# Two expert stages of a fused kernel: own PSUM banks, weights split earlier, an unrolled loop, and column operands in a threshold search

## What is computed

```python
# layer 0: top-2 routing with capacity, 8 experts, 1024 hidden, cap = 640 rows
for e in range(8):
    match = topk_experts == e
    elig = match.any(-1) & ~fallback
    pos = jnp.cumsum(elig) - 1
    kept = elig & (pos < cap); overflow = elig & (pos >= cap)
    idx = ...                       # the tokens that hold slots 0..cap-1
    y_e = gelu(x_flat[idx] @ W1[e] + b1[e]) @ W2[e] + b2[e]
    y_flat = y_flat.at[idx].add(y_e * w[:, None])

# layer 1: expert choice, 8 experts in 4 groups, 682 hidden, 256 tokens for each expert
Sm = softmax(xf @ Wr + br)
G_t, idx_t = jax.lax.top_k(Sm.T, 256)   # each expert takes its 256 best tokens
mid = silu(einsum('keh,ehf->kef', xf[idx], W_up[group]) + b_up[group])
out = einsum('kef,efh->keh', mid, W_down) + b_down
y = zeros.at[idx].add(G[..., None] * out)
```

## Time and profile before

| | |
|---|---|
| median of 3 runs | 868.36 us (865.08 to 871.39) |
| the profiled execution | 871.3 us, of which the span of the trace is 869.6 |
| TensorE busy in the span | 642.2 us, 74% |
| VectorE, ACT, POOL busy | 59%, 48%, 39% |
| mean granted TensorE clock | 0.862 of full speed |

### The profile page before, as it was taken

The page is one execution under the profiler, slowest core; times in us unless marked ns, Lnnn a source line. Parts: engine busy times, 40 slices in busy tenths (PEclk is TensorE's granted clock), DMA queues, the critical chain, the costliest instruction groups (busy, mean ns, idle before and its releaser), DMA issues. The chain is left out here.

```text
span 869.6 us, 14738 instructions
## 1 busy us (share of the span) xinstructions
PE 642.2 (74%) x4856; PEld 475.2 (55%) x4856; DVE 515.6 (59%) x1634; ACT 415.2 (48%) x810; POOL 341.6 (39%) x474
## 2 busy tenths in 40 slices
PE   3988898378999999999424868887778630169895
PEld 3777786247768767877312445554445420047663
DVE  1477656655766575565115577777874438866653
ACT  1355422154775686576111557655656320055672
POOL 2233334364356336552312445344444230123654
PEclk9999999679999999999855789888889755579998
DMA  5253224254455355432311223222200122024543
GB/s 188 75 183 99 74 73 139 75 167 99 122 127 123 86 127 110 136 77 26 55 42 33 62 69 87 72 79 64 73 28 27 50 87 70 8 63 135 147 102 37
DMA packets 73872, 75.94 MB, mean 87 GB/s; under 512 B 8037, under 2 KB 66449, under 8 KB 73553
## 3 DMA queue, kind: packets, MB, share of 16 engines
q1 hardware_dynamic: 61217, 59.32, 21.9%
q0 software_dynamic: 10928, 15.57, 10.3%
q10 hardware_dynamic: 1664, 0.27, 0.2%
HBM read 52.20 MB, written 22.94 MB: 86 GB/s over the span
## 5 line engine op out<-in xcount | busy, mean ns | idle before, releaser
L1866 DVE CUSTOM_DVE_ANT_0 c_sn<-c_ps_s,k_mask 128x128 f32<-128x128 f32 (+1 forms) x256 | 75.8, 352 | 56.1 <-PE c_ps_s L2004 56.1
L1390 PE MATMUL b_ps_y<-b_w2h,b_hh 128*128 128x256 f16 x320 | 87.3, 273 | 6.4 <-DVE b_xl L1283 4.4
L1390 PE MATMUL b_ps_y<-b_w2h,b_hl 128*128 128x256 f16 x320 | 87.2, 273 | 0.0
L1390 PE MATMUL b_ps_y<-b_w2l,b_hh 128*128 128x256 f16 x320 | 87.2, 273 | 0.0
L1698 POOL TENSOR_SCALAR_AFFINE_SELECT c_pr<-c_pr 128x512 f32<-128x512 f32 x64 | 43.2, 675 | 108.6 <-ACT c_pr L1757 107.6
L1200 POOL DMA_INDIRECT res<-b_y,b_s_idx x40 | 69.1, 1727 | 41.7 <-ACT b_y L1242 33.0
L1274 DVE TENSOR_TENSOR b_hl<-b_h,b_hh 128x640 f16<-128x640 f32 x64 | 52.9, 826 | 38.4 <-ACT b_hh L1222 37.7
L1186 POOL DMA_INDIRECT e_xg<-rows,e_g_idx x35 | 37.0, 1056 | 90.9 <-DVE e_g_idx L1301 80.4
L2032 PE MATMUL c_ps_v<-c_pr,k_vx 128*64 128x256 f32 (+1 forms) x512 | 62.4, 369 | 5.6 <-POOL c_pr L1698 5.0
L1355 PE MATMUL b_ps_h<-b_xh,e_w1h 128*128 128x320 f16 x256 | 56.9, 304 | 4.1 <-ACT b_h L1217 3.0
L1757 ACT ACTIVATE c_pr<-c_ps_t 128x768 f32<-128x768 f32 x64 | 51.7, 807 | 13.1 <-PE c_ps_t L2018 13.1
(11 more groups left out here) (409 smaller groups left out, 1776.2 us busy)
## 6 DMA issues: line engine op xcount, KB each, us to landing
e_w<-in_L_ffn_W_dram SPq DMA_DIRECT2D x16, 1024.0 KB, 5.4
d_w<-in_L_ffn_W_down_dram SPq DMA_DIRECT2D x8, 640.0 KB
k_ks<-kT SPq DMA_DIRECT2D x48, 64.0 KB, 3.2
c_qs<-q SPq DMA_DIRECT2D x48, 64.0 KB, 2.3
d_w<-in_L_ffn_W_up_dram SPq DMA_DIRECT2D x4, 682.0 KB, 5.9
rows<-a_rows SPq DMA_DIRECT2D x8, 264.0 KB, 2.6
rows<-c_rows SPq DMA_DIRECT2D x8, 264.0 KB, 2.2
a_x_in<-in_x_dram SPq DMA_DIRECT2D x8, 256.0 KB, 3.3
```

The source lines that it names most:

```text
L1390: last = pe.matmul(ps_y[(j + CT) % 2][:, 0:D], a, b[:, f, :], start=(f == 0 and k == 0), stop=(f == FC - 1 and k == 2))
L1866: dve.tensor_tensor_reduce(sn[r][:, a:b], ps_s[:, r, a:b], mask[:, a:b], -1.0, 3.0e38, ALU.add, ALU.min, mx[g % 2][:, q, r, j:j + 1]).then ...
```

## The change

Capacity experts:

- the turned rows have banks of their own, `ps_x` and `ps_i` in turn, each holding one tile; the index matmuls share `ps_i`, wait for the last xl, and stand behind down tile j=0; VectorE's work on the indices stands behind yb(0);
- W2's split parts are double, and W2 of expert e+1 is split in the down phase of e, a piece behind each of y(0) to y(3); W1's four pieces all stand ahead of yb(0); W2 of expert 0 is split at the end of `attention_causal`; SP loads W1 and W2 an expert further ahead;
- the loop is unrolled.

Expert choice:

- three raw buffers are shared by up and down weights, in one list `WEIGHTS`; there are 3 up and 6 down pairs of split parts; the first seven weights are split while the tokens are selected: ACT scales the raw weight in place and copies it to f16, POOL subtracts; the other five are split in the loop by ACT and VectorE;
- POOL clears only the last 256 columns of each raw buffer; the load of `bd` goes behind the fourth weight and has a semaphore of its own;
- in the threshold search `cand` is made from `more`, `thr` and the next try in one operation with column operands, and `thr` is updated behind it.

```diff
 # attention_causal, end of ACT and of VectorE
+            act.wait_ge(s_w2, 16)
+            for high in down:
+                act.activation(high[1], high[0], ACT.Copy, scale=WS0).then_inc(s_wh2, 1)
...
+            for k, low in enumerate(down):
+                dve.wait_ge(s_wh2, k + 1)
+                dve.scalar_tensor_tensor(out=low[2], in0=low[0], scalar=WS0, in1=low[1], op0=ALU.mult,
+                                         op1=ALU.subtract).then_inc(s_wl2, 1)
 # experts_capacity
-        ps_x = [ps_y[k][:, 0:C * P].rearrange("p (c t) -> p c t", c=C) for k in range(2)]
-        ps_i = pb("ps_i", [P, 512])
+        ps_xi = [pb("ps_x", [P, 2, C, P]), pb("ps_i", [P, 2, C, P])]
+        ps_x = [bank[:, 1, :, :] for bank in ps_xi]
+        IDX = ps_xi[1][:, 0, 0, 0:CT]
...
-                with eng.Fori(0, E // 2 - 1) as i:
-                    step(i * 2, 0, True, True, True)
-                    step(i * 2 + 1, 1, True, True, True)
-                step(E - 2, 0, False, True, True)
-                step(E - 1, 1, False, False, True)
+                for e in range(E):
+                    step(e, e % 2, e + 2 < E, e + 1 < E, True)
 # SP
-                if products and rows:
-                    sp.wait_ge(s_wl2, (e + 1) * WP)
-                    load_down(e + 1)
-                if rows and not (isinstance(e, int) and e + 2 >= E):
+                if rows and e + 2 < E:
                     sp.wait_ge(s_wl1, (e + 2) * WP)
                     load_up(e + 2)
+                    sp.wait_ge(s_wl2, (e + 2) * WP)
+                    load_down(e + 2)
 # ACT, hidden phase, then down phase
-                        if f < WP:
-                            if f == 0:
-                                act.wait_ge(s_w2, (e + 1) * 16)
-                            act.activation(down[f][1], down[f][0], ACT.Copy, scale=WS).then_inc(s_wh2, 1)
...
+                if rows and products:
+                    act.wait_ge(s_w1, (e + 2) * 16)
+                    act.wait_ge(s_ph, (e + 1) * FC)
+                    for part in up:
+                        act.activation(part[1], part[0], ACT.Copy, scale=WS).then_inc(s_wh1, 1)
                 for j in range(CT):
...
+                    if rows and products and j < WP:
+                        if j == 0:
+                            act.wait_ge(s_w2, (e + 2) * 16)
+                        act.activation(down[v][j][1], down[v][j][0], ACT.Copy, scale=WS).then_inc(s_wh2, 1)
 # VectorE, down phase: four w1l pieces, then yb(0), then the indices, then w2l pieces
+                    if slots and j == 0:
+                        dve.wait_ge(s_pidx, e + 3)
+                        dve.tensor_copy(of(who, e + 2), IDX).then_inc(s_who, 1)
...
+                    if rows and products and j < WP:
+                        dve.wait_ge(s_wh2, (e + 1) * WP + j + 1)
+                        dve.scalar_tensor_tensor(out=down[v][j][2], in0=down[v][j][0], scalar=WS, in1=down[v][j][1],
+                                                 op0=ALU.mult, op1=ALU.subtract).then_inc(s_wl2, 1)
 # TensorE
+                def found():
+                    pe.wait_ge(s_vhi, e + 3)
+                    pe.wait_ge(s_atlo, e + 3)
+                    pe.wait_ge(s_xl, (e + 2) * CT)
...
                         if j >= 2:
                             pe.wait_ge(s_yb, e * CT + j - 1)
-                        elif rows:
-                            pe.wait_ge(s_xl, (e + 2) * CT + j - 1)
                         if j == 0:
+                            count(pe, s_yb, e * CT)
                             pe.wait_ge(s_wl2, (e + 1) * WP)
...
+                        if slots and j == 0:
+                            found()
 # experts_choice
+    RAW, UPS, DOWNS, EARLY = 3, 3, 6, 7
+    WEIGHTS = [("up", 0), ("down", 0), ("down", 1), ("up", 1), ("down", 2), ("down", 3),
+               ("up", 2), ("down", 4), ("down", 5), ("up", 3), ("down", 6), ("down", 7)]
...
+            for i in range(len(WEIGHTS)):
+                if i >= RAW:
+                    split_done(sp, i - RAW)
+                load(i)
+                if i == RAW:
+                    sp.dma_start(bd[:], ins["L1_ffn_b_down"].partition_broadcast(P)).then_inc(s_bd, 16)
...
-            for u in range(2):
-                pool.memset(w2[u][:], 0.0).then_inc(s_fill, 1)
+            for u in range(RAW):
+                pool.memset(raw[u][:, FULL * D:FC * D], 0.0).then_inc(s_fill, 1)
...
+            for i in range(EARLY):
+                full, high, low = split_of(i)
+                pool.wait_ge(s_wh, i + 1)
+                pool.tensor_tensor(low, full, high, ALU.subtract).then_inc(s_wlp, 1)
...
+                if i < EARLY:
+                    act.activation(full, full, ACT.Copy, scale=WS).then_inc(s_wsc, 1)
+                    act.wait_ge(s_wsc, i + 1)
+                    act.activation(high, full, ACT.Copy).then_inc(s_wh, 1)
+                else:
+                    act.activation(high, full, ACT.Copy, scale=WS).then_inc(s_wh, 1)
...
-                    dve.tensor_tensor(cand[:], thr[:], tries[:, n:n + 1], ALU.bitwise_or).then_inc(s_cand, 1)
...
+                    given = tries[:, n + 1:n + 2]
+                    if n:
+                        dve.tensor_scalar(cand[:], more[:], thr[:], given, ALU.bitwise_or, ALU.bitwise_or)\
+                            .then_inc(s_cand, 1)
...
-                    dve.tensor_tensor(thr[:], thr[:], more[:], ALU.bitwise_or).then_inc(s_thr, 1)
+                if n:
+                    dve.tensor_scalar(thr[:], more[:], thr[:], None, ALU.bitwise_or).then_inc(s_thr, 1)
...
-                if e >= 0:
-                    down_low(e)
...
-                if e >= 0 and e % 2 == 0 and group(e + 2) < G:
-                    up_low(group(e + 2))
+                if 0 <= e < len(WEIGHTS) - EARLY:
+                    weights_low(EARLY + e)
...
-            pe.wait_ge(s_ldb, 48)
+            pe.wait_ge(s_ldb, 32)
```

More of the change, by code:

```diff
@@ L99, in capacity_tables @@
              "w1h": sb("w1h", [P, C, F], F16), "w1l": sb("w1l", [P, C, F], F16),
+             "w2h": [sb(f"w2h{u}", [P, FC, D], F16) for u in range(2)],
+             "w2l": [sb(f"w2l{u}", [P, FC, D], F16) for u in range(2)],
              "at_lo": [sb(f"at_lo{u}", [P, NT, P], F16) for u in range(2)],
@@ L231, in attention_causal @@
                                "w2", "w1h", "w1l", "at_lo", "at_hi", "vhi", "g_idx", "xg"))
-        up = pieces(w1, w1h, w1l)
+        up, down = pieces(w1, w1h, w1l), pieces(w2, tiles["w2h"][0], tiles["w2l"][0])
         ps_x, ps_c, ps_q, ps_k, ps_v, ps_w, ps_s, ps_p = (
@@ L1096, in run @@
                 step(-1, 1, False, True, False)
-                with eng.Fori(0, E // 2 - 1) as i:
-                    step(i * 2, 0, True, True, True)
-                    step(i * 2 + 1, 1, True, True, True)
-                step(E - 2, 0, False, True, True)
-                step(E - 1, 1, False, False, True)
+                for e in range(E):
+                    step(e, e % 2, e + 2 < E, e + 1 < E, True)
             return run
         def count(eng, what, value):
-            if not isinstance(value, int) or value > 0:
+            if value > 0:
                 eng.wait_ge(what, value)
         WP = WP0
-        up, down = pieces(w1, w1h, w1l), pieces(w2, w2h, w2l)
-        assert WP <= CT and WP <= FC
+        up, down = pieces(w1, w1h, w1l), [pieces(w2, w2h[u], w2l[u]) for u in range(2)]
+        assert WP <= CT and CT % 2 == 1 and E % 2 == 0
         block = ctx.enter_context(nc.Block(no_gpsimd_drain=True))
@@ L1310, in step @@
                                              op0=ALU.add, op1=ALU.add).then_inc(s_si, 1)
+                if rows and products:
+                    for k, part in enumerate(up):
+                        dve.wait_ge(s_wh1, (e + 1) * WP + k + 1)
+                        dve.scalar_tensor_tensor(out=part[2], in0=part[0], scalar=WS, in1=part[1], op0=ALU.mult,
+                                                 op1=ALU.subtract).then_inc(s_wl1, 1)
                 for j in range(CT):
-                    if rows and products and j < WP:
-                        dve.wait_ge(s_wh1, (e + 1) * WP + j + 1)
-                        dve.scalar_tensor_tensor(out=up[j][2], in0=up[j][0], scalar=WS, in1=up[j][1], op0=ALU.mult,
-                                                 op1=ALU.subtract).then_inc(s_wl1, 1)
                     if products:
@@ L2229, in rows_of, with raw_count, split_of, split_done @@
             return P if f < FULL else LAST
+        def raw_count(i):
+            return sum(16 if WEIGHTS[k][0] == "up" else 32 for k in range(i % RAW, i + 1, RAW))
+        def split_of(i):
+            kind, n = WEIGHTS[i]
+            if kind == "up":
+                return raw[i % RAW][:, 0:C * F], wide(w1h[n % UPS]), wide(w1l[n % UPS])
+            return raw[i % RAW][:], wide(w2h[n % DOWNS]), wide(w2l[n % DOWNS])
+        def split_done(eng, i):
+            if i < EARLY:
+                eng.wait_ge(s_wlp, i + 1)
+            else:
```

(11 more changed lines are left out.)

186 lines of the change are left out of this document (79 added, 107 removed).

## The result

The changed kernel takes 843.37 us (median of 4, 842.57 to 844.16) against 868.01 for before: a ratio of 0.9715, 95% interval 0.9678 to 0.9752. It is 24.6 us faster; 847 was forecast, with 838 to 860 as the range.

What follows compares the result with a forecast made beforehand. TensorE was taken to bound the capacity loop (169.4 us busy of 179). Terms summed to -20.7 us, from the median 868.36 to 847.7, stated as 847; own range 838 to 856, 838 to 860 with (c), (b) and most of mild (a).

Steps and rivals of the forecast that it cites:

- Attention's end: End of the attention ahead of the capacity experts: gains the first expert's four down pieces, +0.5 us, bounds 0 and +2.5.
- Experts 1 to 6: Capacity loop: TensorE waits of 9.5 us removed, 2 back as a new wait on yb(0); net -7.5 us.
- Expert 0: Capacity stage, first expert: waits on b_xl (1.3) and b_yb (1.7, put to the loop's first pass) go; -3.0 us.
- Ahead of the threshold: Choice stage: shorter memsets bring the copy of scores earlier, biases' transpose waits less; -2.5 us, bounds -1.5 and -2.7.
- Threshold: Choice stage, eight-level search: the OR making cand leaves the chain, 0.1 to 0.19 us for each of seven; -1.0 us.
- POOL splits in the selection: Choice stage: for up to 5 us POOL runs beside two-input operations behind the search; +2 us, bounds 0 and +5.
- Choice loop: Choice stage: TensorE waits on d_w2l (4.5) and d_h (4.4) go, 1 us unseen; -8.5 us, bounds -4 and -11.
- Rival (a): Capacity loop: POOL's gathers and scatters become the limit; mild 848 to 866 us, chance 0.10; a loss, 877, 0.04.
- (b): Choice stage, threshold search: POOL holds up one-column operations, some 13 us lost, 2 saved behind; 858 us, chance 0.09.
- (c): Choice loop: half of the 8.9 us comes back as waits on d_xg; 852 us, chance 0.10.

Runs made afterwards that it cites:

- choice half alone: Kernel before with only the expert choice stage changed, capacity stage as before: 854.0 us, ratio 0.9848.
- loop written out alone: Kernel before with the capacity loop over pairs of experts written out and nothing else changed: 867.2 us, ratio 0.9993.
- long fills: Changed kernel with the 1536-column clears of two raw buffers and the early load of the down biases, as before: 843.2 us, ratio 0.9717.
- capacity half alone: Changed kernel's capacity part with the expert choice stage of before: 857.8 us, ratio 0.9888 to before.
- added wait: Changed kernel where TensorE's hidden phase of expert 5 in the choice stage waits for an added transfer: 849.2 us, ratio 0.9803 to before.
- old threshold: Changed kernel with the threshold search of before, cand and thr made by two-input operations from SBUF: 853.0 us, ratio 0.9802 to before.

## Why the prediction was right, and where it was off

The direction, the range and the places were right; 20.7 were summed, 24.6 came. The nearness of the sum is partly luck: by the medians of the halves the capacity stage gave less than its 10.7 (8.9) and the choice stage more than its 10.0 (12.7), though both forecasts lie within the intervals. Term by term, forecast and then what the profiles or the controlled runs have:

- **Attention's end**, +0.5: +0.1. The splits run beside the gather. The +4.6 of the whole attention is no part of the change: it varies by 8 us among kernels with the same code there, with stretches of half clock at different places.
- **Experts 1 to 6**, -7.5: -10.2 against the profile of before, -8.7 against the choice half alone. The removed waits were right, 4.6 and 3.8 by the earlier trace rows, and the table load went with the loop. The 2 us booked for a new wait on yb(0) did not come, but only just. VectorE had yb(0) ready (0.42 from 263.62) just as TensorE wanted the bank, and down j=2 started at 264.09:

```profile
...
261.21 2.49 DVE L1305 SCALAR_TENSOR_TENSOR e_w1l<-e_w,e_w1h 128x512 f16<-128x512 f32 x4
263.62 0.42 DVE L1312 SCALAR_TENSOR_TENSOR b_yb<-b_ps_y,e_b 128x256 f32<-128x256 f32 x1
...
```

```profile
...
264.09 0.28 PE L1398 MATMUL b_ps_y<-e_w2h,b_hh 128*128 128x256 f16 x1
...
```

  TensorE came later than I had it (near 5.8 to 6) and VectorE sooner (6.4): down j=0, found and j=1 took until 6.16 us into the phase and yb(0) came at 6.1, the same in each of these experts. TensorE is idle 0.09 us ahead of that matmul in experts 1 to 5, and 0.6 us in expert 6, which has no found; the 0.6 is all that the view counts. So there is no slack left here.
- **Expert 0**, -3.0: -5.0 against the profile of before, -3.1 against the choice half alone. The step that failed is its reason. The 1.7 us of the earlier trace rows was put to the loop's first pass; the choice half alone has the loop and not that wait, and its expert 0 took 33.9 us. The Trainium skill's rule on fetching behind a taken branch (page "Runtime: NRT & Kernel Launch", section "Instruction fetch mechanics"), cited for it, is borne out by no run here. What gave the 3.1 instead: 1.4 by the loop written out alone (33.9 to 32.5), by the table load, which I had given no price, and 1.7 by the place of W2 (32.5 to 30.8). Why yb(0) was late in that one execution was not looked for.
- **Ahead of the threshold**, -2.5: -2.6. The term is right where it stands; by the long fills only 0.7 of it reaches the end of the stage.
- **Threshold**, -1.0: -0.6. The new `cand` takes 0.27 us, the old one 0.159, so less of the chain went than the 0.19 of a step. VectorE's timeline has it, an `ok` and the first operation behind the search:

```profile
...
708.79 0.27 DVE L2457 TENSOR_SCALAR d_cand<-d_more,d_thr,d_tries 128x1 int32<-128x1 int32 x1
708.98 0.20 DVE L2462 TENSOR_SCALAR d_thr<-d_more,d_thr 128x1 int32<-128x1 int32 x1
...
711.49 0.16 DVE L2444 TENSOR_SCALAR d_ok<-d_cnt 128x1 f16<-128x1 f32 x1
...
729.01 1.19 DVE L2466 COPY d_thr_row<-d_thr 128x128 f32<-128x128 f32 x1
```

- **POOL splits in the selection**, +2: +0.9. POOL was done at 730.1, 1.1 us behind the search, not 5; its subtractions took 2.78 and 3.08 us, 2.0 ns a column where the earlier trace rows had 2.26:

```profile
...
709.24 6.16 POOL L2320 TENSOR_TENSOR d_w2l<-d_raw,d_w2h 128x1536 f16<-128x1536 f32 x2
...
727.35 2.77 POOL L2320 TENSOR_TENSOR d_w1l<-d_raw,d_w1h 128x1364 f16<-128x1364 f32 x1
```

  Its last one held the copy of 128x128 behind the search: 1.19 us, against 0.227 in before.
- **Choice loop**, -9.5 on TensorE and 1 back in the tail: -15.1 and 2.0 back between the two profiles. The waits went as named, 4.5 and 4.4 of the earlier trace rows; those on d_xg and d_xl stayed, 3.2 and 3.1. The term that was mis-sized is the clock. I gave it 0.6 us, for which I named no row, and between these profiles it was 5.8: the busy time of the same 700 matmuls, 82.0 to 76.2. Before had three stretches of 3.4 us at half clock inside the loop, at 782.6, 826.9 and 857.7, each behind waits; this is the first:

```profile
...
782.60:786.00 3.40, 3.28 (x30) 2.66 (x31) 2.50 (x4) 1.97 (x2) 0.00 (x0) 0.50 0.67 205
...
```

  But this is the price of that execution and not of the waits. The loop written out alone has the choice stage of before, and its profile has the same waits (5.3 and 4.8 us in place of 4.5 and 4.4), 15.1 us of idle time in all in place of 14.0, and half clock only in the first 4.4 us of the choice loop. Its whole loop, then the 3.4 us behind its longest wait:

```profile
...
763.54:855.95 92.41, 77.27 (x700) 59.27 (x700) 56.27 (x78) 59.12 (x105) 43.99 (x26) 0.98 0.41 98
...
800.20:803.60 3.40, 2.54 (x33) 1.95 (x33) 2.49 (x3) 3.31 (x8) 3.10 (x2) 1.00 0.32 39
...
```

```profile
...
PE d_ps_t L2586 <- ACT d_h L2341: 4.8, 2, 3.4
...
```

  Against this execution the loop is 11.4 us shorter, 10.4 of it idle time and 1.0 busy time, and the tail is the same (8.8 and 8.9 us). So 9.3 to 10.4 us of idle time is what the change takes from this loop, as forecast by the 8.9, and the clock gives 1.0 to 6.3 us on top, by which execution of the old loop stands for before: the capacity half alone, whose choice stage is also that of before, again has three stretches and is busy 82.5 us. That TensorE's waits bring the half clock is likely (the added wait had 3.1 us of it behind it); what decides which of them do was not looked for.

**Rival (a)** did not come: no transposes wait for e_xg, no wait for res. **(b)** did not come either, and the old threshold says why it might have: an operation with two inputs from SBUF was held even at one column, and `ok`, with one input of one column, was not. That agrees with the Trainium skill's page "SBUF — State Buffer", section "Who interferes with whom", on two inputs; whether a tensor_scalar of one column is held, it leaves to conditions on the operands, and here `ok` took 0.157 us in every level. One input is no safeguard at more columns: the operation of the earlier trace rows, which the prediction put beside the two-input ones, has one input, and so have the copy of 128x128 and the copy of the gate, 128x5, which took 5.12 us beside POOL's fills. So the column operands were no small gain of 0.6 but the condition for POOL's splits: without them the search is 8.5 us longer and the choice stage 7.0. I had priced only the 0.16 us. **(c)**, waits with a new name, did not come: d_xg 3.2 us after 3.6.

The same holds for found: I priced its move as free, covered by down j=0. It is free there, and costs 18.7 us ahead of the down product, now that it shares a bank with the turned rows. The forecast came out right with the gains of own banks (2.9), W2's place (8.2) and the loop (2.6), which add up to 13.7, against 12.7 measured from the choice half alone.

## What to carry to other kernels

Where a wait is taken off TensorE, look at the granted clock in the stretch behind it: the busy time of the work that follows can be part of the price. Take that part from more than one execution, since here the same loop of before was 5.8 us busier than the changed one in one execution and 1.0 in another. Before work is given to POOL, go through what VectorE does beside it, and reckon with every operation with two inputs from SBUF, and every copy or tensor_scalar of more than one column, being held for a whole POOL instruction or more, however small it is. An idle stretch with a single occurrence, like the 1.7 us of expert 0, is worth a second execution before it is given a cause.

## What was not expected of the hardware

A VectorE operation of one column and two inputs took 3.02 us beside POOL's subtraction, and 0.16 without; a copy of five columns took 5.12 us beside POOL's fills, and 0.16 with the fills put off. The same code took 177 to 185 us in the first attention: the shortest, 177.3, had two stretches of half clock of 3.4 us in it, the longest, 185.5, had five. They do not account for all of it, since another with two took 181.1. What decides where they fall was not looked for. Matmuls whose result nobody reads raised the granted clock from 0.5 (1.2 GHz) to 1.0 (2.4 GHz) before the rows came, so that hidden 0 behind them took 4.1 us in place of 6.3. At the capacity stage fewer of them, with a pause in between, did nothing; why is left open.
